# Sharing a convolution tap of every second chunk between ACT and GpSimd in a state-space scan (one core, fp32)

## The chip, the core and the metric

The kernel runs on one core of a Trainium2 chip. Its time is the device time of one execution in microseconds. The names of the engines are those of the profile: PE is TensorE, DVE is VectorE, ACT is ScalarE, POOL is GpSimd, and SP issues most of the DMAs. Each engine works through its own queue in order; they meet through semaphores.

## The reference

Eight sequences of 256 tokens of width 256 go through two layers. The part that matters here is the mixer of the first layer. Each token is projected to x (256 channels), B and C (32 heads of 64 states each) and a few more. The channels of x, B and C go through a causal convolution of four taps along the sequence:

```
def causal_conv1d(x, w, b):   # y[t] = w3 x[t] + w2 x[t-1] + w1 x[t-2] + w0 x[t-3] + b
```

Then comes the scan: with the running sums cum of the decays, each head takes scores[i, j] = exp(cum[i] - cum[j]) * (C[i] . B[j]) for j <= i, zero otherwise, and y = scores x. Gates, an output projection, a feed-forward block, LoRA experts, attention and a mixture of experts follow; the change does not touch them.

## The kernel before, in words

The 2048 tokens are worked in four rounds (`for r in range(ROUNDS)`) of 512 tokens, two sequences of 256. Channels lie on the partitions, tokens along the free axis, so that one chunk of 128 channels is a tile of 128x512. A head pair p (16 of them) needs two chunks of the convolution: ("BC", p, 0), the B channels of two heads, and ("BC", p, 1), the C channels. They are kept in `bc`, three pairs deep (`p % 3`), in SBUF.

The scan of a round has 32 steps, `steps[g]`, a head pair p and a sequence b each: (0,0), (0,1), (1,0), (1,1) and so on up to pair 13, then (14,0), (15,0), (14,1), (15,1). What each engine does in step g is written out by hand, one loop for each engine (the taps of the first two pairs come before the scan):

- SP (`broadcast_rows`, L793 to L804) loads the rows of running sums of step g into one of four buffers `crow[g % 4]`, and for that waits until the decays of step g-4 are done.
- POOL (L1529 to L1537) waits for that load and puts 1e30 above the diagonal with two `affine_select`, one per head. This is the mask; it counts up `masked`. POOL does nothing else in the scan.
- ACT (L1411 to L1416) takes `decay(g + 1)`, four exponentials over `crow` that wait for the masks of step g+1, and then `first_tap` for the chunk that PE projects in step g: out of PSUM, times the last tap's weight, plus the bias, into `bc`.
- PE (L1055 to L1076) takes the products C.B of step g (L1032, L1033), the projection of one chunk (`project_bc(p + 2, b)`: four matmuls of 128x512, L883), and in every second step `add_y` (L1048, L1051), which multiplies the scores with x. A projection goes to PSUM bank b, and for that the chunk before in that bank must be drained. The products of a pair wait until both of its chunks are drained.
- DVE (L1858 to L1880) multiplies the decays with the products (L1871, the score multiplication), then takes taps 2 and 3 of the chunk of step g-1, and then tap 1 of the chunk of step g. A tap (L1651) is one `scalar_tensor_tensor` that reads the projection from PSUM, shifted by s tokens, and adds it to `bc`; tap 1 waits for ACT's first tap, tap 3 drains the bank. At g = 20 and g = 31 half of the output and a quarter of it are written in front of the score multiplication (`output`, L1848, L1855).

Of the kernel before, what the change touches and what calls it, by code (L numbers as in the profile page):

```python
# [107 lines left out]
def sandwich(nc, A, out):  # L108
    with ExitStack() as ctx:
# [9 lines left out]
        def settle(eng):  # L119


            eng.sem_inc(settled, 1)
# [96 lines left out]

        sg = xc  # L220

        lg0 = sb("lg0", [P, TILES, EXPERTS0])
        mx = sb("mx", [P, TILES, 8])
        ix = sb("ix", [P, TILES, 8], U32)
# [172 lines left out]
        cum_ready = signal("cum_ready", 1)  # L397
        cum_out = sem("cum_out")
        crow_in = [sem(f"crow_in{i}") for i in range(CROWS)]
        decayed = signal("decayed", 64)  # L400
        masked = signal("masked", 64)
        y_added = signal("y_added", 64)
# [519 lines left out]
        def _(pe):  # L922
# [67 lines left out]
            for r in range(ROUNDS):  # L990
# [64 lines left out]
                for g in range(2 * PAIRS):  # L1055
                    p, b = steps[g]
                    ns = (2 * g, 2 * g + 1)
                    if b == 0:
                        for w in range(2):
                            pe.wait_ge(*plan.drained(("BC", p, w), r))  # L1060
                    pe.wait_ge(*plan.before(("CB", p, b), r))
                    for second in [products(n) for n in ns]:
                        mm = second()
                    mm.then_inc(plan.fills(("CB", p, b)), 1)
                    if p + 2 < PAIRS:
                        if p + 2 == PROJ_PAIRS[1] and b == 0:
                            pe.wait_ge(w_proj[2], 16)
                        project_bc(p + 2, b)
                    if g == 1:

                        for c in range(DC):
                            pe.wait_ge(*plan.before(("Y", c), r))
                            pe.matmul(plan[("Y", c)][:, :], zeros_bf[:, 0:P], zeros_bf[:, :], start=True,
                                      stop=False, skip_group_check=True).then_inc(plan.fills(("Y", c)), 1)
                    if g >= 1 and steps[g - 1][0] % 2 == 1:
                        add_y(*steps[g - 1])  # L1076
# [237 lines left out]
        def _(act):  # L1314
# [48 lines left out]
            for r in range(ROUNDS):  # L1363
                def first_tap(key, dst, j):
                    act.wait_ge(*plan.full(key, r))
                    act.activation(dst, plan[key][:, :], ACT.Identity, bias=conv_b[:, j:j + 1],  # L1366
                                   scale=conv_w[:, j, TAPS - 1:TAPS]).then_inc(tap0.sem, 1)

                for c in range(DC):
                    first_tap(("X", c), xc[:, c, :], c)  # L1370
                for w in range(2):
# [39 lines left out]
                for g in range(2 * PAIRS):  # L1411
                    p, b = steps[g]
                    if g + 1 < 2 * PAIRS:
                        decay(g + 1)
                    if p + 2 < PAIRS:
                        first_tap(("BC", p + 2, b), bc[:, (p + 2) % 3, b, :], 2 + 16 * b + p + 2)  # L1416

                if r > 1:
                    act.wait_ge(sh_out, 16 * (r - 1) + CREDIT)
# [69 lines left out]
        @block.gpsimd  # L1489
        def _(pool):  # L1490
            def power(n, cols, r):
                pool.wait_ge(var_ready.sem, var_ready.at(r, n))
                pool.tensor_tensor(rs[:, cols], ve[:, cols], half[:, cols], ALU.pow).then_inc(rstd_ready.sem, 1)  # L1493

            def ahead_power(r, n):
                pool.wait_ge(ahead_var.sem, ahead_var.at(r, n))
                pool.tensor_tensor(rs1[:, :], ve1[:, :], half[:, :], ALU.pow).then_inc(ahead_rstd.sem, 1)

            pool.memset(half[:, :], -0.5).then_inc(pads_zero, 1)
            pool.wait_ge(pads_zero, 1)  # L1500
            ahead_power(0, 1)
            ahead_power(0, 2)
            pool.memset(x_pad[:, :, :], 0.0).then_inc(pads_zero, 1)
            pool.memset(v_pad[:, :, :, :, :], 0.0).then_inc(pads_zero, 1)
            pool.memset(before[:, :, :], 0.0).then_inc(pads_zero, 1)
            pool.memset(xf[:, :, :], 0.0).then_inc(pads_zero, 1)
            pool.memset(table[:, :, :], 0.0).then_inc(pads_zero, 1)
            pool.memset(nmax[:, :, :, :], 0.0).then_inc(pads_zero, 1)
            for e in range(2):
                pool.memset(head_ones[:, e, 16 * e:16 * e + 16], 1.0).then_inc(pads_zero, 1)  # L1510
            pool.memset(head_ones[:, :, :].rearrange("p e d -> p (e d)")[:, 16:48], 0.0).then_inc(pads_zero, 1)
            pool.wait_ge(pads_zero, PADS)

            def spread_rows(d):
                pool.wait_ge(groups_ready.sem, groups_ready.at(d, 1))
                settle(pool)
                for h in range(2):
                    pool.tensor_tensor(oh_rows[:, :, h, :], in_group[:, :, :], row_parts[:, h, :].unsqueeze(2)
                                       .broadcast_to([P, TILES * TOPK, EGROUPS]), ALU.mult)\
                                           .then_inc(rows_ready.sem, 1)  # L1520
                pool.wait_ge(rows_ready.sem, rows_ready.at(d, 2))
                settle(pool)
                pool.tensor_scalar(row_parts[:, 0, :], row_parts[:, 0, :], float(GROUP * TOPK // 64), None, ALU.add)\
                    .then_inc(row_chain.sem, 1)
                pool.wait_ge(row_chain.sem, row_chain.at(d, 1))
                settle(pool)

            for r in range(ROUNDS):
                for g in range(2 * PAIRS):  # L1529

                    pool.wait_ge(crow_in[g % CROWS], (r * (2 * PAIRS // CROWS) + g // CROWS) * 16 + 16)
                    settle(pool)
                    for e in range(2):
                        diagonal = crow[g % CROWS][:, e, :].rearrange("p (b l) -> p b l", l=P)[:, 0:3:2, :]
                        pool.affine_select(diagonal, diagonal, pattern=[[0, 2], [1, P]], base=0,
                                           channel_multiplier=-1, compare_op=ALU.is_ge,
                                           fill=1e30).then_inc(masked.sem, 1)  # L1537
                def keep_causal(ks):


                    for k in ks:
                        pool.wait_ge(*plan.drained(("ST", k), r))
                        settle(pool)
                        for i in range(2):
                            x = prT[k % 6][:, i, 0:SEQ].rearrange("p (b n) -> p b n", n=P)
                            pool.affine_select(x, x, pattern=[[0, 2], [1, P]], base=0, channel_multiplier=-1,
                                               compare_op=ALU.is_ge, fill=0.0).then_inc(causal.sem, 1)

                att = len(POWERS) - 4
                for n in range(att):  # L1550
                    power(n + 1, POWERS[n], r)
                    if n == 1 and r > 0:
                        spread_rows(r - 1)
                keep_causal((0, 1))
                if r < LAST:
                    ahead_power(r + 1, 1)
                keep_causal((2,))
                if r < LAST:
                    ahead_power(r + 1, 2)
                keep_causal(range(3, 14))  # L1560
                power(att + 1, POWERS[att], r)
                keep_causal((14, 15))
                for n in range(att + 1, att + 4):
                    power(n + 1, POWERS[n], r)
            spread_rows(LAST)
            tail_pool(pool)
# [3 lines left out]
        def _(dve):  # L1570
# [69 lines left out]
            def tap(r, s, chunks, taps_done):  # L1640
# [7 lines left out]
                for n, (key, dst, j) in enumerate(chunks):  # L1648
                    d = dst.rearrange("p (b l) -> p b l", b=SEQS)[:, :, s:SEQ]
                    x = plan[key][:, :].rearrange("p (b l) -> p b l", b=SEQS)[:, :, 0:SEQ - s]  # L1650
                    ins = dve.scalar_tensor_tensor(d, x, conv_w[:, j, TAPS - 1 - s:TAPS - s], d,  # L1651
                                                   ALU.mult, ALU.add)
                    if s < TAPS - 1:
                        ins.then_inc(chain, 1)
                        count[0] += 1
                        last_tap[0] = count[0]
                    else:
                        ins.then_inc(plan.drains(key), 1)

            last_tap = [0]  # L1660

# [115 lines left out]
            for r in range(ROUNDS):  # L1777
# [80 lines left out]
                for g in range(2 * PAIRS):  # L1858
# [15 lines left out]
                    if g == 0:  # L1874
                        tap(r, TAPS - 1, [bc_chunk(1, w) for w in range(2)], taps_done)
                    if g >= 1 and (g - 1) // SEQS + 2 < PAIRS:
                        tap(r, 2, [bc_chunk((g - 1) // SEQS + 2, (g - 1) % SEQS)], taps_done)
                        tap(r, 3, [bc_chunk((g - 1) // SEQS + 2, (g - 1) % SEQS)], taps_done)
                    if p + 2 < PAIRS:
                        tap(r, 1, [bc_chunk(p + 2, b)], taps_done)  # L1880
                output(1, slice(SEQ, GROUP), 64)

# [330 lines left out]
```

## Time and profile before

| | us |
|---|---|
| median of 3 runs | 1291.43 (1290.85 to 1294.38) |
| the profiled execution, its own time | 1297.54 |
| its span, first to last instruction | 1295.5 |
| PE busy | 1110.3 (86% of the span) |
| DVE busy | 867.8 (67%) |
| ACT busy | 499.0 (39%) |
| POOL busy | 251.8 (19%) |
| mean granted clock of TensorE | 0.939 of full speed |

The shares are averages over stages that have different limits, so they say little about one stage. The span is 2.0 us shorter than the execution's own time, because it counts from the first instruction to the last. A granted clock of 1.00 is 2.4 GHz and one of 0.50 is 1.2 GHz.

### The profile page before, as it was taken

Reading aid. Unit: us, or ns where it says so; the run is one execution under the profiler, and the core shown is the slowest. Engines: PE = TensorE matmul, PEld = TensorE weight load, DVE = VectorE, ACT = ScalarE, POOL = GpSimd, SP = SyncE. Lnnn points to the kernel's source line nnn. Section 1 sums busy time; section 2 is a strip of 40 time slices with the busy share of each in tenths; the row PEclk is TensorE's granted clock in tenths of the full one; section 3 lists DMA queues with packets and bytes.
Section 4 is the critical chain, followed back from the end, with each engine's and each line's share of the span. In section 5 each row is a group of like instructions: output and inputs, shape, how many; then the busy total and the mean of one; then the engine's idle time right before and its main releaser. Section 6 shows DMA issues by size and latency. Waiting matters only on the chain.

```text
span 1295.5 us, 19826 instructions
## 1 busy us (share of the span) xinstructions
PE 1110.3 (86%) x7192; PEld 672.5 (52%) x7192; DVE 867.8 (67%) x1848; ACT 499.0 (39%) x1076; POOL 251.8 (19%) x522
## 2 busy tenths in 40 slices
PE   3999896888998997888998997888998997886667
PEld 1444554554445675554445674554445675465345
DVE  5899526669997545669996636769997546565126
ACT  2766411236665202246665102236664111221133
POOL 3222001132221000222221000222221000222432
PEclk9999998899999997899999997899999997897679
DMA  5888100004431000004331000004348030035345
GB/s 177 284 266 282 36 1 16 1 2 133 120 116 59 1 8 26 2 2 146 121 120 41 1 17 17 1 5 155 122 123 216 4 94 21 2 81 167 118 162 186
DMA packets 72673, 111.75 MB, mean 86 GB/s; under 512 B 5896, under 2 KB 62608, under 8 KB 71682
## 3 DMA queue, kind: packets, MB, share of 16 engines
q1 hardware_dynamic: 68738, 98.51, 24.4%
q10 hardware_dynamic: 2304, 8.39, 2.0%
q0 software_dynamic: 1536, 3.60, 0.9%
q8 instruction: 57, 0.93, 0.3%
q14 instruction: 38, 0.31, 0.1%
HBM read 91.81 MB, written 19.27 MB: 86 GB/s over the span
## 4 chain that ended last, share of the span: by engine, by line
PE 61%; DVE 20%; issue 7%; ACT 6%; DMA 2%; another core or an unknown queue 1%; POOL 1%; DVEq 0%; SPq 0%; POOLq 0%; ACTq 0%
PE bank L883 22%; DVE hf L1651 5%; PE bank L948 4%; PE bank L1124 4%; PE bank L1165 3%; PE bank L1032 3%; PE bank L1048 2%; DVE nmax L2041 2%; PE bank L962 2%; PE bank L1211 2%; DVE u L1871 2%; PE bank L1208 2%; PE bank L896 2%; DMA out_dram<-tmp 2%
## 5 line engine op out<-in xcount | busy, mean ns | idle before, releaser
L883 PE MATMUL bank<-uT,w_in 128*128 128x512 f32 (+1 forms) x584 | 288.2, 621 | 25.0 <-DVE hf L1651 11.3
L1651 DVE SCALAR_TENSOR_TENSOR hf<-bank,conv_w,hf 128x510 f32<-128x510 f32 (+2 forms) x384 | 277.9, 743 | 18.5 <-ACT hf L1366 13.3
L883 PEld LDWEIGHTS bank<-uT,w_in 128*128 128x128 f32 (+1 forms) x584 | 99.9, 188 | 123.3 <-issue 90.1
L1366 ACT ACTIVATE hf<-bank,conv_b,conv_w 128x512 f32<-128x512 f32 x128 | 99.4, 777 | 136.6 <-PE bank L883 136.6
L1493 POOL TENSOR_TENSOR rs<-ve,half 128x2 f32<-128x2 f32 x56 | 39.0, 697 | 382.1 <-DVE ve L1783 382.1
L1032 PE MATMUL bank<-hf 64*128 64x256 f32 x512 | 89.7, 426 | 12.6 <-issue 7.2
L883 PE MATMUL bank<-uT,w_gu 128*128 128x512 f32 x224 | 99.0, 593 | 0.0
L2041 DVE TENSOR_REDUCE nmax<-bank 128x2 f32<-128x256 f32 (+1 forms) x128 | 65.4, 554 | 44.1 <-PE bank L1211 44.1
L1032 PEld LDWEIGHTS bank<-hf 64*128 64x128 f32 x512 | 38.8, 184 | 69.8 <-issue 63.5
L1871 DVE TENSOR_TENSOR turned_p<-dec,bank 128x768 f32<-128x768 f32 x64 | 60.9, 952 | 15.9 <-PE bank L1033 5.0
L1346 ACT ACTIVATE xc<-bank 128x512 f32<-128x512 f32 x44 | 26.3, 597 | 115.3 <-PE bank L883 77.1
L883 PEld LDWEIGHTS bank<-uT,w_gu 128*128 128x128 f32 x224 | 42.3, 190 | 46.6 <-issue 45.9
L1901 DVE TENSOR_TENSOR hf<-xc,bank 128x512 f32<-128x512 f32 x32 | 22.0, 687 | 62.8 <-PE bank L883 44.6
L1124 PE MATMUL bank<-w_dn,hf 128*128 128x256 f32 x256 | 56.2, 380 | 3.6 <-issue 3.6
L948 PE MATMUL bank<-uT_moe,w_sgu 128*128 128x256 f32 x256 | 58.7, 384 | 0.0
L874 PE MATMUL bank<-ident,u 128*128 128x128 f32 x128 | 23.9, 318 | 39.6 <-DVE u L1607 17.1
L948 PEld LDWEIGHTS bank<-uT_moe,w_sgu 128*128 128x128 f32 x256 | 49.6, 194 | 12.1 <-issue 5.7
L1124 PEld LDWEIGHTS bank<-w_dn,hf 128*128 128x128 f32 x256 | 48.3, 190 | 13.2 <-issue 6.8
L1033 PEld LDWEIGHTS bank<-hf 64*128 64x128 f32 x512 | 50.0, 187 | 5.3
L1463 ACT ACTIVATE dec<-bank 128x768 f32<-128x768 f32 x32 | 26.0, 811 | 64.2 <-PE bank L1222 64.2
L1463 ACT ACTIVATE turned_p<-bank 128x768 f32<-128x768 f32 x24 | 19.5, 811 | 80.6 <-PE bank L1222 80.6
L1033 PE MATMUL bank<-hf 64*128 64x128 f32 x512 | 49.9, 270 | 0.0
(314 smaller groups left out, 2174.9 us busy)
## 6 DMA issues: line engine op xcount, KB each, us to landing
hf<-cum_dram SPq DMA_DIRECT2D x32, 384.0 KB, 3.7
dec<-cum_dram SPq DMA_DIRECT2D x32, 384.0 KB, 3.6
tmp<-cum_dram SPq DMA_DIRECT2D x32, 384.0 KB, 3.6
x<-cum_dram SPq DMA_DIRECT2D x32, 384.0 KB, 3.5
y_dram<-xf SPq DMA_DIRECT2D x16, 512.0 KB
hf<-y_dram ACTq DMA_DIRECT2D x16, 512.0 KB, 4.5
w_in<-in_w_in SPq DMA_DIRECT2D x1, 3584.0 KB, 12.0
w_in<-in_w_egu SPq DMA_DIRECT2D x6, 512.0 KB, 9.2
```

Of the source, the lines that this page charges most:

```text
L883: mm = pe.matmul(plan[key][0:n, :], w[:, k, cols], uT[:, k, :], start=k == 0, stop=k == DC - 1)
L948: mm = pe.matmul(plan.of(key, d)[:, i * HALF:(i + 1) * HALF], w_sgu[:, k, o + i * P:o + (i + 1) * P], uT_moe[:, k, j * HALF:(j + 1) * HALF ...
L1032: pe.matmul(cb[:, e, 0:SEQ], B[:, o:o + P], C[:, o:o + SEQ], start=True, stop=True)
L1033: return lambda: pe.matmul(cb[:, e, SEQ:TRI], B[:, o + P:o + SEQ], C[:, o + P:o + SEQ], start=True, stop=True)
L1124: mm = pe.matmul(plan[("F", j)][:, i * D:(i + 1) * D], hf[:, f, t * P:(t + 1) * P], w_dn[:, f, :], start=f == 0, stop=f == FF // P - 1)
L1165: mm = pe.matmul(plan[key][:, cols], w_att[:, k, n, c * P:(c + 1) * P], uT[:, k, cols], start=k == 0, stop=k == DC - 1)
L1366: act.activation(dst, plan[key][:, :], ACT.Identity, bias=conv_b[:, j:j + 1], scale=conv_w[:, j, TAPS - 1:TAPS]).then_inc(tap0.sem, 1)
L1463: act.activation(prT[k % 6], pair_banks(("ST", k))[:, :, 0:TRI], ACT.Exp)\
L1493: pool.tensor_tensor(rs[:, cols], ve[:, cols], half[:, cols], ALU.pow).then_inc(rstd_ready.sem, 1)
L1651: ins = dve.scalar_tensor_tensor(d, x, conv_w[:, j, TAPS - 1 - s:TAPS - s], d, ALU.mult, ALU.add)
L1871: dve.tensor_tensor(sc[g % 4], dec[:, d:d + 2, :], both_cb[g % 2][:, :, 0:TRI], ALU.mult).then_inc(plan.drains(("CB", p, b)), 1)
L2041: ins = dve.tensor_reduce(nmax[:, n // 4 % 2, i, col:col + 33:32], S[:, :, cols], AX.X, ALU.max, negate=True)
```

## The change

For each C chunk of pairs 2 to 15 (b = 1, 14 a round) the tap furthest back, tap 3, leaves DVE. ACT multiplies the projection with the tap's weight right behind `first_tap` of the same chunk, into a buffer `last_product` (a part of `yg`, one buffer for all chunks, so from the second chunk of a round on ACT waits for the addition of the chunk before). POOL adds this product to the chunk in SBUF; it does so in the even steps g from 2 to 28, behind the mask of step g and in front of the mask of step g+1, for the chunk that PE projects in step g-1, and it waits for ACT's product and for DVE's last tap of that chunk. DVE takes taps 1 and 2 of such a chunk both in step g, and tap 2 drains the bank. The B chunks keep their order. PE waits for the addition before the products of a pair (`conv_sum`).

```diff
--- before.py
+++ after.py
@@ -218,6 +218,8 @@
         cum_tok = sb("cum_tok", [P, TILES, HEADS])
 
         sg = xc
+
+        last_product = yg[:, 1, :].rearrange("p (b l) -> p b l", b=SEQS)[:, :, TAPS - 1:SEQ]
 
         lg0 = sb("lg0", [P, TILES, EXPERTS0])
         mx = sb("mx", [P, TILES, 8])
@@ -397,6 +399,8 @@
         cum_ready = signal("cum_ready", 1)
         cum_out = sem("cum_out")
         crow_in = [sem(f"crow_in{i}") for i in range(CROWS)]
+        tap3 = signal("tap3", PAIRS - 2)
+        conv_sum = signal("conv_sum", PAIRS - 2)
         decayed = signal("decayed", 64)
         masked = signal("masked", 64)
         y_added = signal("y_added", 64)
@@ -1058,6 +1062,8 @@
                     if b == 0:
                         for w in range(2):
                             pe.wait_ge(*plan.drained(("BC", p, w), r))
+                        if p >= 2:
+                            pe.wait_ge(conv_sum.sem, conv_sum.at(r, p - 1))
                     pe.wait_ge(*plan.before(("CB", p, b), r))
                     for second in [products(n) for n in ns]:
                         mm = second()
@@ -1366,6 +1372,14 @@
                     act.activation(dst, plan[key][:, :], ACT.Identity, bias=conv_b[:, j:j + 1],
                                    scale=conv_w[:, j, TAPS - 1:TAPS]).then_inc(tap0.sem, 1)
 
+                def tap_product(p):
+
+                    key = ("BC", p, 1)
+                    if p > 2:
+                        act.wait_ge(conv_sum.sem, conv_sum.at(r, p - 2))
+                    x = plan[key][:, :].rearrange("p (b l) -> p b l", b=SEQS)[:, :, 0:SEQ - TAPS + 1]
+                    act.activation(last_product, x, ACT.Copy, scale=conv_w[:, 18 + p, 0:1]).then_inc(tap3.sem, 1)
+
                 for c in range(DC):
                     first_tap(("X", c), xc[:, c, :], c)
                 for w in range(2):
@@ -1414,6 +1428,8 @@
                         decay(g + 1)
                     if p + 2 < PAIRS:
                         first_tap(("BC", p + 2, b), bc[:, (p + 2) % 3, b, :], 2 + 16 * b + p + 2)
+                        if b == 1:
+                            tap_product(p + 2)
 
                 if r > 1:
                     act.wait_ge(sh_out, 16 * (r - 1) + CREDIT)
@@ -1535,6 +1551,14 @@
                         pool.affine_select(diagonal, diagonal, pattern=[[0, 2], [1, P]], base=0,
                                            channel_multiplier=-1, compare_op=ALU.is_ge,
                                            fill=1e30).then_inc(masked.sem, 1)
+                    p = (g - 2) // SEQS + 2
+                    if g >= 2 and g % 2 == 0 and p < PAIRS:
+
+                        pool.wait_ge(tap3.sem, tap3.at(r, p - 1))
+                        pool.wait_ge(*plan.drained(("BC", p, 1), r))
+                        settle(pool)
+                        x = bc[:, p % 3, 1, :].rearrange("p (b l) -> p b l", b=SEQS)[:, :, TAPS - 1:SEQ]
+                        pool.tensor_tensor(x, x, last_product, ALU.add).then_inc(conv_sum.sem, 1)
                 def keep_causal(ks):
 
 
@@ -1657,6 +1681,14 @@
                     else:
                         ins.then_inc(plan.drains(key), 1)
 
+            def tap_and_drain(r, s, key, dst, j):
+
+                dve.wait_ge(chain, last_tap[0])
+                d = dst.rearrange("p (b l) -> p b l", b=SEQS)[:, :, s:SEQ]
+                x = plan[key][:, :].rearrange("p (b l) -> p b l", b=SEQS)[:, :, 0:SEQ - s]
+                dve.scalar_tensor_tensor(d, x, conv_w[:, j, TAPS - 1 - s:TAPS - s], d, ALU.mult, ALU.add)\
+                    .then_inc(plan.drains(key), 1)
+
             last_tap = [0]
 
             def sum_dt(r):
@@ -1874,9 +1906,15 @@
                     if g == 0:
                         tap(r, TAPS - 1, [bc_chunk(1, w) for w in range(2)], taps_done)
                     if g >= 1 and (g - 1) // SEQS + 2 < PAIRS:
-                        tap(r, 2, [bc_chunk((g - 1) // SEQS + 2, (g - 1) % SEQS)], taps_done)
-                        tap(r, 3, [bc_chunk((g - 1) // SEQS + 2, (g - 1) % SEQS)], taps_done)
-                    if p + 2 < PAIRS:
+                        p2, b2 = (g - 1) // SEQS + 2, (g - 1) % SEQS
+                        if b2 == 0:
+                            tap(r, 2, [bc_chunk(p2, b2)], taps_done)
+                            tap(r, 3, [bc_chunk(p2, b2)], taps_done)
+                        else:
+                            dve.wait_ge(tap3.sem, tap3.at(r, p2 - 1))
+                            tap(r, 1, [bc_chunk(p2, b2)], taps_done)
+                            tap_and_drain(r, 2, *bc_chunk(p2, b2))
+                    if p + 2 < PAIRS and b == 0:
                         tap(r, 1, [bc_chunk(p + 2, b)], taps_done)
                 output(1, slice(SEQ, GROUP), 64)
 
```

## Rows read from the trace of the kernel before

**Rows 1.** The page's head.
```profile
span 1295.5 us, 19826 instructions
```

**Rows 2.** Stretch table: us, busy PE, PEld, DVE, ACT, POOL, granted clock, DMA
```profile
315.20:412.00 96.80, 91.21 (x600) 46.30 (x600) 90.06 (x121) 64.53 (x152) 21.51 (x56) 1.00 0.37 115
```

**Rows 3.** The chain that ended last, round 1: start us, us, engine, tile, line
```profile
388.87 1.98 PE bank L883 x4
390.85 0.57 PE bank L1048 x8
391.42 0.22 PE bank L1051 x8
391.64 0.63 PE bank L1032 x4
392.27 0.22 PE bank L1033 x4
392.50 1.91 PE bank L883 x4
```

**Rows 4.** DVE timeline, round 1: start us, us, line, operation, count
```profile
321.00 0.94 DVE L1871 TENSOR_TENSOR u<-dec,bank 128x768 f32<-128x768 f32 x1
...
379.11 0.74 DVE L1848 SCALAR_TENSOR_TENSOR yg<-xc,chan,bank 128x512 f32<-128x512 f32 x1
...
380.50 0.95 DVE L1871 TENSOR_TENSOR turned_p<-dec,bank 128x768 f32<-128x768 f32 x1
...
387.30 2.18 DVE L1651 SCALAR_TENSOR_TENSOR hf<-bank,conv_w,hf 128x508 f32<-128x508 f32 x3
389.39 0.94 DVE L1871 TENSOR_TENSOR h<-dec,bank 128x768 f32<-128x768 f32 x1
...
392.60 0.95 DVE L1871 TENSOR_TENSOR turned_p<-dec,bank 128x768 f32<-128x768 f32 x1
393.47 1.52 DVE L1651 SCALAR_TENSOR_TENSOR hf<-bank,conv_w,hf 128x508 f32<-128x508 f32 x2
395.26 0.75 DVE L1651 SCALAR_TENSOR_TENSOR hf<-bank,conv_w,hf 128x510 f32<-128x510 f32 x1 [0.27 <-ACT hf L1366]
...
405.64 0.95 DVE L1871 TENSOR_TENSOR turned_p<-dec,bank 128x768 f32<-128x768 f32 x1
...
410.03 0.95 DVE L1871 TENSOR_TENSOR u<-dec,bank 128x768 f32<-128x768 f32 x1
```

**Rows 5.** ACT's timeline in the same stretch
```profile
394.45 0.78 ACT L1366 ACTIVATE hf<-bank,conv_b,conv_w 128x512 f32<-128x512 f32 x1 [1.39 <-PE bank L883]
395.13 0.50 ACT L1405 ACTIVATE dec<-tmp,cum_tok 128x256 f32<-128x256 f32 x1
...
395.82 0.49 ACT L1405 ACTIVATE dec<-tmp,cum_tok 128x256 f32<-128x256 f32 x1
```

**Rows 6.** POOL's timeline in the same stretch
```profile
386.98 0.77 POOL L1535 TENSOR_SCALAR_AFFINE_SELECT tmp<-tmp 128x256 f32<-128x256 f32 x2 [2.74 <-DMA tmp<-cum_dram]
```

**Rows 7.** Groups by form, POOL, then ACT: count, busy us, mean ns, idle
```profile
L1518 POOL TENSOR_TENSOR oh_rows<-in_group,row_parts 128x256 bf16<-128x256 f32 x8 | 4.8, 623 | 74.4 <-DVE in_group L1728 74.4
...
L1523 POOL TENSOR_SCALAR row_parts<-row_parts 128x16 f32<-128x16 f32 x4 | 1.0, 262 | 0.8 <-POOL oh_rows L1518 0.8
...
L1366 ACT ACTIVATE hf<-bank,conv_b,conv_w 128x512 f32<-128x512 f32 x128 | 99.4, 777 | 136.6 <-PE bank L883 136.6
...
L1322 ACT ACTIVATE uT<-bank 128x512 f32<-128x512 f32 x16 | 9.5, 595 | 72.2 <-PE bank L874 72.2
```

**Rows 8.** Timeline of a handoff from DVE to POOL, after the scan
```profile
474.57 0.17 DVE L1783 TENSOR_SCALAR ve<-mv 128x2 f32<-128x2 f32 x1
474.82 0.72 POOL L1493 TENSOR_TENSOR rs<-ve,half 128x2 f32<-128x2 f32 x1 [32.15 <-DVE ve L1783]
```

**Rows 9.** Stretch table, PE's pause behind the scan of round 1
```profile
418.40:420.40 2.00, 0.84 (x6) 0.47 (x5) 1.11 (x5) 0.68 (x4) 0.74 (x2) 1.00 0.00 0
...
420.80:424.40 3.60, 3.60 (x12) 3.03 (x13) 0.62 (x2) 2.12 (x3) 0.00 (x0) 0.55 0.00 0
```

## The prediction

> Notation: step g of the scan is what each engine does for steps[g]; c(g) is the chunk projected in step g (even g: a B chunk, b = 0; odd g: a C chunk, b = 1).
>
> **What bounds it now.** I read the page's head, then the stretch table, the chain, and last the timelines of one engine at a time. The profiled execution has a span of 1295.5 us [rows 1]. The scan of round 1 fills 96.8 us of it and the other three look the same: PE is busy for 91.21 us, DVE for 90.06, at 2.4 GHz throughout (granted clock 1.00) [rows 2]. So two engines are nearly full, and a tap less on DVE looks like a gain. The chain says how much: it alternates between DVE and long stretches of PE, so PE has almost nothing to give. A projection takes PE 1.91 to 1.98 us, the products 0.63 + 0.22, a Y addition 0.57 + 0.22 [rows 3]. A pair of steps holds two projections, two pairs of products and one addition: 2 x 1.92 + 2 x 0.85 + 0.79 = 6.33 us. The real pace is (405.64 - 321.00) / 13 = 6.51 us per pair, from the score multiplication (L1871) of step 2 to that of step 28 [rows 4]. With DVE for nothing the scan could win 0.18 us a pair.
>
> The distances from which I build [rows 4]: score multiplication to the first tap behind it 0.87 us (392.60 to 393.47); tap to tap 0.70 (three from 387.30 to 389.39); two taps to the end of the second 1.52. ACT [rows 5]: from a decay's first exponential to what follows the fourth 1.38 (two heads of 0.69 each, 395.13 to 395.82), a first tap 0.78, and 0.03 from its end (395.23) to the DVE tap that waits for it (395.26).
>
> What nobody waits for today is POOL. Its masks run far ahead: the mask of step 26 starts at 386.98 [rows 6], and ACT reads it at 395.13 [rows 5], while DVE is only between steps 22 and 23. That lead of 8.1 us is what the change spends.
>
> **The change, part by part.**
> DVE loses tap 3 of one chunk in each pair: 14 a round, 0.70 us each, 39 us in 56 pairs. At most 0.18 of each 0.70 could have counted.
>
> ACT gains 14 products a round, 128x506 from PSUM. Not in the trace; bounds are the plain copy of 128x512, 0.595, and the tap with scale and bias, 0.777 [rows 7]. I take 0.68. It stands behind first_tap(g) of odd steps, before a decay whose cover is good for more than that (below), so it costs nothing here; without that cover it would be up to 0.78 x 56 = 44 us.
>
> POOL gains 14 additions a round of 128x506 f32 with two inputs. The nearest two-input row is L1518, 128x256, 0.623 us; a 128x16 operation takes 0.262 [rows 7]. So 0.262 + 506 / 256 x (0.623 - 0.262) = 0.97 us. Below, it is not cheaper than a mask of half its size with one input, 0.41; above, not more than twice L1518, 1.25. L1518 does not have the addition's shape, so both ends stay in the range.
> The Trainium skill (GPSIMD Engine Reference, section 3.1) speaks against this move: elementwise work with two inputs is about twice as slow on GpSimd, 4497 ns for 2048 f32 columns; that would make the addition some 1.11 us by an estimate, and the sum 8 us longer.
>
> The price lies in where the addition stands. POOL's queue is in order: mask(g), then for even g from 2 to 28 the wait for DVE's last tap of c(g-1), the addition, and only then mask(g+1). DVE issues that last tap in step g, behind the score multiplication of g. So queued behind POOL's new wait is mask(g+1); behind it on ACT decay(g+1); behind that, in ACT's order, first_tap(g); and for that waits DVE's tap 1 of c(g), which in DVE's order stands before the score multiplication of g+1. This is a loop through three engines, without slack. From the start of the score multiplication of an even g:
> - tap 1 and tap 2 of c(g-1): 0.87 + 1.52 = 2.39
> - to POOL 0.08, as a small DVE result reaches POOL today (474.74 to 474.82) [rows 8], and the addition 0.97: 3.44
> - first half of mask(g+1) 0.41, to ACT 0.03: 3.88
> - decay(g+1) 1.38: 5.26
> - first_tap(g) 0.78, to DVE 0.03: 6.07
> - tap 1 of c(g) 0.70: 6.77, score multiplication of g+1 0.87: 7.64
> - tap 2 and tap 3 of c(g) 1.40: 9.04, and the next pair begins.
> So 9.04 us a pair instead of 6.51.
>
> Is anything else late in such a pair? decay(g+2) runs on ACT from 6.04 to 7.4, and first_tap(g+1) and the product from 7.4 to 8.9, before the 9.9 at which DVE asks for them. PE waits for conv_sum until 3.44, in front of the products of g+2, which nobody needs before 9.04. PE's projection of c(g+2) waits for the bank, which tap 3 of c(g) frees at about 9.1; then PE has 6.33 us of work in 9.04 and stands still for 2.7. SP's row loads for step g+4 go out after decay(g), as today, and are masked more than a pair later; they remain hidden, though all masks are late.
>
> Per round: 13 pairs x 9.04 = 117.5 in place of 84.64. Once a round DVE writes half of the output before step 20, 1.39 us (379.11 to 380.50) [rows 4]; it stands in the loop now and adds all of it: 118.9, so +34.3. From step 28 to 30: decay(29) ends at about 5.3, decay(30) behind it at 6.7, so the score multiplication of 30 stands at 6.74 instead of 410.03 - 405.64 = 4.39 [rows 4]: +2.35. Step 1 loses a tap before the loop begins: -0.70. Sum 35.9, in four rounds 144 us. Nothing outside the scan changes.
>
> The profiled execution took 1297.5 us, 6 above the median of the runs, and would take 1441; from the median, 1291.4 + 144 = **1435 us**.
>
> **Rivals.**
> - *The clock falls and PE becomes the bound.* After 2.00 us in which PE was busy for 0.84 at a granted clock of 1.00, a stretch of 3.6 us had 0.55 on average, near 1.2 GHz [rows 9]. The new gap of 2.7 us is of that kind. One such fall, 3.6 to 4 us long, costs PE some 2 us of work, less than its 2.7 us of slack, so I charge nothing. If it lasted for the whole of every pair, PE would need 12.66 us a pair: 52 x 3.62 = 188 more, 1623 us; in half of the pairs, about 1529. Against that: PE is dense for over 6 us once it starts, and the 0.55 is above 0.50, so the clock rose again before that stretch was over, in which PE was busy throughout [rows 9]. Chance 0.08. [...]
> - *The addition is much dearer than L1518 suggests*, 2 us say: 56 x 1.03 = 58 more, 1493 us. Chance 0.05.
> - *Faster: POOL stays ahead.* The taps, the product and the addition all lie beside PE's work, and PE bounds at 6.33: 52 x 0.18 = 9 us less, 1282. It decides if mask(g+1) is there when ACT asks for it. ACT begins a decay before DVE begins the step in front of it; by my table the mask comes 3.85 us after that begins. For it stand DVE's and PE's shares of the scan; against it, the order of POOL's queue. Chance 0.03; that the two effects cancel to no change (within 0.3%, about what a measurement of this kernel can tell) 0.02.
>
> **Numbers.** Forecast 0.82: 1435 us, and from 1404 (addition 0.41: 56 x 0.56 less) to 1451 (1.25: 56 x 0.28 more). Handoffs that I left out, 0.05 to 0.2 us a pair, add up to 11, and clock falls that reach the loop in part take it further. The range goes from 1404 to 1495; that leaves out the faster cases, the worst of the clock and a little of the rest. Slower by over 0.3%: 0.95, the same 0.02, faster 0.03.
>
> **What would show it.** Score multiplications in pairs of 9 us, the shorter part (about 2.3) after odd steps, the longer (6.8) after even ones. POOL's masks of odd steps directly behind the new addition, whose wait is put down to DVE's tap; a long wait of ACT's exponentials for POOL masks, and of DVE's tap 1 for ACT's first tap. POOL in the chain, in which it hardly appears now. PE's share of the scan falls from 94% to about 70%. Wrong if the masks of odd steps still run a step ahead of ACT; if the pair is PE from end to end; or if the addition takes well over 1.25 us.

## The result, and the profile after

| | before | changed | ratio |
|---|---|---|---|
| median of 4 runs, us | 1291.14 | 1454.66 | 1.127 (1.123 to 1.131) |

The change costs 163.5 us; 144 were predicted (1435 us), the range of 1404 to 1495 holds the result. I follow the profile in the order in which the prediction was built. The page's head first: its span and the busy time of each engine.

```profile
span 1452.9 us, 20030 instructions
...
PE 1161.8 (80%) x7172; PEld 692.9 (48%) x7192; DVE 829.2 (57%) x1792; ACT 525.3 (36%) x1132; POOL 315.6 (22%) x578
```

DVE has become 39 us less busy, as meant (867.8 before), and the span 157 us longer. An engine that is freed without being what the others wait for gives nothing back. PE's busy time grew by 51 us although its work is the same: that is the lower clock, below. In the chain that ended last PE's share fell from 61% to 42%, and those of DVE (20% to 27%), ACT (6% to 14%) and POOL (1% to 3%) grew.

The stretch table, with the same columns as [rows 2]. First the 13 pairs of round 1; then the pair of that round in which the clock was lowest and which took longest (the pair with half of the output aside), one in which it did not fall, one in which it fell for a shorter part, and the last pair, in which it did not fall either.

```profile
364.07:487.53 123.46, 96.23 (x536) 44.80 (x536) 70.16 (x94) 62.31 (x143) 35.05 (x65) 0.89 0.25 82
392.16:401.72 9.56, 9.38 (x41) 4.24 (x41) 5.37 (x9) 4.46 (x11) 2.69 (x5) 0.67 0.28 89
401.72:411.09 9.37, 6.33 (x40) 3.09 (x40) 5.29 (x7) 5.21 (x12) 2.70 (x5) 1.00 0.23 77
411.09:420.46 9.37, 8.01 (x40) 3.47 (x40) 5.28 (x8) 4.78 (x11) 2.70 (x5) 0.82 0.25 80
...
478.17:487.53 9.36, 7.25 (x56) 3.56 (x56) 5.27 (x8) 4.77 (x11) 2.70 (x5) 1.00 0.23 80
```

From step 2 to step 28 a round takes 123.46 us instead of 84.64 [rows 4]. An undisturbed pair takes 9.37 us (9.04 predicted), and in it PE is busy for 6.33, the work that the prediction had added up for it (most pairs at full clock read 6.39). No engine is full: the pair is a chain of waits. Here it is, DVE's timeline of that pair:

```profile
401.72 0.95 DVE L1903 TENSOR_TENSOR u<-dec,bank 128x768 f32<-128x768 f32 x1
402.59 0.74 DVE L1675 SCALAR_TENSOR_TENSOR hf<-bank,conv_w,hf 128x510 f32<-128x510 f32 x1
403.37 0.75 DVE L1689 SCALAR_TENSOR_TENSOR hf<-bank,conv_w,hf 128x508 f32<-128x508 f32 x1
408.13 0.75 DVE L1675 SCALAR_TENSOR_TENSOR hf<-bank,conv_w,hf 128x510 f32<-128x510 f32 x1 [4.01 <-ACT hf L1372]
408.79 0.94 DVE L1903 TENSOR_TENSOR h<-dec,bank 128x768 f32<-128x768 f32 x1
409.65 1.52 DVE L1675 SCALAR_TENSOR_TENSOR hf<-bank,conv_w,hf 128x508 f32<-128x508 f32 x2
411.09 0.94 DVE L1903 TENSOR_TENSOR turned_p<-dec,bank 128x768 f32<-128x768 f32 x1
```

then POOL's timeline, and ACT's:

```profile
404.29 1.26 POOL L1561 TENSOR_TENSOR hf<-hf,yg 128x506 f32<-128x506 f32 x1 [6.88 <-DVE hf L1689]
405.50 0.77 POOL L1551 TENSOR_SCALAR_AFFINE_SELECT x<-x 128x256 f32<-128x256 f32 x2
```

```profile
405.94 0.51 ACT L1419 ACTIVATE dec<-x,cum_tok 128x256 f32<-128x256 f32 x1 [3.79 <-POOL x L1551]
...
407.33 0.76 ACT L1372 ACTIVATE hf<-bank,conv_b,conv_w 128x512 f32<-128x512 f32 x1
```

L1903 is the score multiplication, L1675 a tap, L1689 the last tap of a C chunk, L1561 the addition, L1551 the mask, L1419 the first of the exponentials, L1372 the first tap. Read across: DVE ends tap 2 at 404.12; POOL, which had nothing to do for 6.88 us, adds; the mask of the next step follows; ACT has waited 3.79 us for it; behind the decay comes the first tap, for which DVE has waited 4.01 us. The next score multiplication stands 7.07 us after the one before, and the one behind it 2.30 us later: the long and the short part of the pair that the prediction gave as 6.8 and 2.3.

The groups by line show the two new operations, and the waits show that this happens in nearly every pair (56 additions):

```profile
L1561 POOL TENSOR_TENSOR hf<-hf,yg 128x506 f32<-128x506 f32 x56 | 70.3, 1256 | 412.9 <-DVE hf L1689 412.9
...
L1381 ACT ACTIVATE yg<-bank,conv_w 128x506 f32<-128x506 f32 x56 | 37.5, 670 | 0.0
```

```profile
DVE hf L1675 <- ACT hf L1372: 211.6, 56, 4.0
...
ACT dec L1419 <- POOL dec L1551: 134.6, 28, 6.0
ACT dec L1419 <- POOL x L1551: 124.2, 28, 4.7
```

### The profile page after: what moved, and what is told of

It is laid out like the page before. It is cut to its first block, busy times and chain, and to the rows that moved or that the text cites. A ratio compares the mean times of both kernels' runs of the same rounds, so it can differ in the third digit from the quotient of the medians.

```text
span 1452.9 us, 20030 instructions
## 1 busy us (share of the span) xinstructions
PE 1161.8 (80%) x7172; PEld 692.9 (48%) x7192; DVE 829.2 (57%) x1792; ACT 525.3 (36%) x1132; POOL 315.6 (22%) x578
## 4 chain that ended last, share of the span: by engine, by line
PE 42%; DVE 27%; ACT 14%; issue 11%; POOL 3%; DMA 2%; POOLq 1%; DVEq 0%; SPq 0%; ACTq 0%
PE bank L887 11%; DVE hf L1675 6%; ACT dec L1419 4%; PE bank L952 4%; ACT dec L1421 4%; DVE turned_p L1903 3%; PE bank L1130 3%; DVE hf L1689 3%; PE bank L1171 3%; ACT hf L1372 3%; DVE nmax L2079 2%; DVE h L1903 2%; PE bank L1217 2%; PE bank L966 2%; PE bank L1214 1%
## 5 line engine op out<-in xcount | busy, mean ns | idle before, releaser
L887 PE MATMUL bank<-uT,w_in 128*128 128x512 f32 (+1 forms) x584 | 321.8, 683 | 118.0 <-DVE hf L1675 105.9
L1675 DVE SCALAR_TENSOR_TENSOR hf<-bank,conv_w,hf 128x510 f32<-128x510 f32 (+2 forms) x272 | 199.8, 743 | 214.8 <-ACT hf L1372 211.6
L887 PEld LDWEIGHTS bank<-uT,w_in 128*128 128x128 f32 (+1 forms) x584 | 107.6, 202 | 226.5 <-DVE hf L1675 116.5
L1561 POOL TENSOR_TENSOR hf<-hf,yg 128x506 f32<-128x506 f32 x56 | 70.3, 1256 | 412.9 <-DVE hf L1689 412.9
L1036 PE MATMUL bank<-hf 64*128 64x256 f32 x512 | 99.8, 469 | 23.9 <-POOL hf L1561 18.6
L1372 ACT ACTIVATE hf<-bank,conv_b,conv_w 128x512 f32<-128x512 f32 x128 | 97.8, 764 | 24.2 <-PE bank L887 24.1
L1036 PEld LDWEIGHTS bank<-hf 64*128 64x128 f32 x512 | 43.6, 207 | 88.3 <-issue 82.0
L1419 ACT ACTIVATE dec<-dec,cum_tok 128x256 f32<-128x256 f32 x64 | 32.0, 499 | 134.6 <-POOL dec L1551 134.6
L1419 ACT ACTIVATE dec<-x,cum_tok 128x256 f32<-128x256 f32 x64 | 32.0, 499 | 124.2 <-POOL x L1551 124.2
L1903 DVE TENSOR_TENSOR turned_p<-dec,bank 128x768 f32<-128x768 f32 x64 | 60.5, 946 | 19.0 <-PE bank L1037 14.3
L1037 PEld LDWEIGHTS bank<-hf 64*128 64x128 f32 x512 | 54.7, 205 | 7.6
```

Of the source, the lines that this page charges most:

```text
L887: mm = pe.matmul(plan[key][0:n, :], w[:, k, cols], uT[:, k, :], start=k == 0, stop=k == DC - 1)
L1036: pe.matmul(cb[:, e, 0:SEQ], B[:, o:o + P], C[:, o:o + SEQ], start=True, stop=True)
L1037: return lambda: pe.matmul(cb[:, e, SEQ:TRI], B[:, o + P:o + SEQ], C[:, o + P:o + SEQ], start=True, stop=True)
L1419: act.activation(dec[:, n % 4, 0:SEQ], crow[g % CROWS][:, e, 0:SEQ], ACT.Exp, bias=cum_tok[:, 2 * b, h:h + 1], scale=-1.0)
L1561: pool.tensor_tensor(x, x, last_product, ALU.add).then_inc(conv_sum.sem, 1)
L1903: dve.tensor_tensor(sc[g % 4], dec[:, d:d + 2, :], both_cb[g % 2][:, :, 0:TRI], ALU.mult).then_inc(plan.drains(("CB", p, b)), 1)
```

## Experiments

The theory to be tested: the time is the loop DVE's last tap, POOL's addition, mask, ACT's decay, ACT's first tap, DVE's tap 1, and it exists only because of the order in POOL's queue. The rival: it is the added work itself, on ACT and POOL, or what it does to the others in SBUF. Two of the kernels leave a part of the computation out; their expectations say which. The ratios are to the kernel before as it ran beside each experiment: 1289.0 us for the first four kernels below, 1290.2 us for the last three.

**POOL takes the addition three masks later** (changed kernel):

```diff
-                    p = (g - 2) // SEQS + 2
-                    if g >= 2 and g % 2 == 0 and p < PAIRS:
+                    h = g - 3
+                    p = (h - 2) // SEQS + 2
+                    if h >= 2 and h % 2 == 0 and p < PAIRS:
```

> POOL takes each addition three steps later in its own order, behind the mask of step g+3 instead of that of step g; all the work of the change stays. Loop theory (mask of g+1 stuck behind the addition): the loop is gone, PE bounds the pair at 6.33 us, about 1282 us. Load theory (the time is the added work on ACT and POOL, or their traffic in SBUF): the work is the same, so it stays above 1400 us.

Measured: 1289.5 us, ratio to the kernel before 1.000 (0.998 to 1.002). All of the 163 us are gone with the work unchanged. The load theory is out. The expected 1282 us did not come; the time is 7 us above it. Its DVE timeline, the score multiplications of steps 14, 16 and 18 of round 1, and POOL's timeline:

```profile
360.41 0.95 DVE L1904 TENSOR_TENSOR u<-dec,bank 128x768 f32<-128x768 f32 x1 [0.38 <-PE bank L1037]
...
366.73 0.95 DVE L1904 TENSOR_TENSOR turned_p<-dec,bank 128x768 f32<-128x768 f32 x1 [0.61 <-PE bank L1037]
...
373.06 0.95 DVE L1904 TENSOR_TENSOR u<-dec,bank 128x768 f32<-128x768 f32 x1 [0.38 <-PE bank L1037]
```

```profile
344.01 1.27 POOL L1562 TENSOR_TENSOR hf<-hf,yg 128x506 f32<-128x506 f32 x1 [2.67 <-DVE hf L1690]
345.24 0.76 POOL L1551 TENSOR_SCALAR_AFFINE_SELECT hf<-hf 128x256 f32<-128x256 f32 x2
```

Two pairs in 12.65 us: 6.32 each, and what DVE waits for are PE's products (L1037). So PE bounds the pair, at the value predicted for that case. The 13 pairs of a round take 82.5 us instead of 84.64. What was won there is lost at the end of the round: the four last score multiplications spread over 10.12 us in round 1 (9.08 to 10.12 in the four rounds) instead of 6.38. DVE's and PE's timelines of that place, and two stretches:

```profile
404.67 0.95 DVE L1904 TENSOR_TENSOR turned_p<-dec,bank 128x768 f32<-128x768 f32 x1 [0.61 <-PE bank L1037]
...
414.79 0.95 DVE L1904 TENSOR_TENSOR h<-dec,bank 128x768 f32<-128x768 f32 x1 [0.59 <-PE bank L1037]
```

```profile
408.74 1.22 PE L1036 MATMUL bank<-hf 64*128 64x256 f32 x4 [3.39 <-POOL hf L1562]
```

```profile
404.00:406.00 2.00, 1.35 (x24) 0.77 (x20) 1.39 (x3) 1.97 (x6) 0.72 (x2) 1.00 0.00 0
...
410.00:412.00 2.00, 2.00 (x16) 1.46 (x18) 1.19 (x2) 0.46 (x2) 0.00 (x0) 0.50 0.00 0
```

Step 29 is the first of head pair 15, whose C chunk is the last one added. There is no projection left to fill the time, so PE stands still for 3.39 us until that addition is there, and the granted clock falls to 0.50, that is 1.2 GHz. In the kernel before, PE stood still for 1.81 us in front of the same products, and the clock stayed at 1.00:

```profile
408.14 0.70 PE L1032 MATMUL bank<-hf 64*128 64x256 f32 x4 [1.81 <-issue]
```

**One mask later only** (the same edit with `h = g - 1`):

> The addition one step later only, between the mask of g+1 and that of g+2. Loop theory: the mask of g+2 would come 4.2 us after the score multiplication of g, ACT asks for it at about 5.3, so nothing is late: about 1282 us, the same as with three masks ahead. Rival (any coupling of POOL to DVE's taps is harmful): between 1300 and 1400 us. Load theory: above 1400 us.

Measured: 1291.5 us, ratio 1.002 (1.000 to 1.003); 1282 were expected, and again the end of the round is what is missing. One mask ahead is as good as three within 0.2%, and nothing of the loop is left (the 13 pairs take 82.9 us): tying POOL to DVE's taps does no harm as long as the next mask is out first. This kernel also happens to separate the two parts of the end of a round. PE's wait for the last addition was as long in round 1 as in round 2 (PE's timeline), but of these two only in round 1 did the clock fall in the stretch from step 28 to step 31 (stretch table); it fell in rounds 0 and 1 and not in 2 and 3:

```profile
409.35 1.23 PE L1036 MATMUL bank<-hf 64*128 64x256 f32 x4 [3.39 <-POOL hf L1562]
...
696.19 0.70 PE L1036 MATMUL bank<-hf 64*128 64x256 f32 x4 [3.40 <-POOL hf L1562]
```

```profile
405.27:415.19 9.92, 6.53 (x57) 4.56 (x50) 5.17 (x7) 5.00 (x14) 2.69 (x5) 0.66 0.01 2
692.11:700.07 7.96, 4.12 (x57) 3.00 (x50) 5.00 (x7) 5.00 (x14) 2.69 (x5) 1.00 0.01 2
```

Against 6.38 us before, the wait is worth 1.6 us, and the clock another 2.0 where it falls.

**The addition cut to 8 of 506 columns** (changed kernel):

```diff
-                        x = bc[:, p % 3, 1, :].rearrange("p (b l) -> p b l", b=SEQS)[:, :, TAPS - 1:SEQ]
-                        pool.tensor_tensor(x, x, last_product, ALU.add)
+                        x = bc[:, p % 3, 1, :].rearrange("p (b l) -> p b l", b=SEQS)[:, :, TAPS - 1:TAPS + 3]
+                        pool.tensor_tensor(x, x, last_product[:, :, 0:4], ALU.add)
```

> As the changed kernel, but POOL adds only the first 4 columns of each sequence (8 of 506), so most of tap 3 of the C chunks is left out; every wait stays. Loop theory: the addition falls from 1.26 to about 0.26 us and each of 56 loops gets shorter by it: 56 us less, about 1398 us. If the addition were covered: no change, 1455 us.

Measured: 1400.1 us, ratio 1.087 (1.083 to 1.090), 54.6 less than the changed kernel. The group of the addition and two score multiplications of even steps on DVE's timeline:

```profile
L1561 POOL TENSOR_TENSOR hf<-hf,yg 128x8 f32<-128x8 f32 x56 | 11.6, 206 | 411.3 <-DVE hf L1689 411.3
```

```profile
365.37 0.94 DVE L1903 TENSOR_TENSOR u<-dec,bank 128x768 f32<-128x768 f32 x1
...
373.70 0.95 DVE L1903 TENSOR_TENSOR turned_p<-dec,bank 128x768 f32<-128x768 f32 x1
```

The addition is 1.05 us shorter and the pair 1.04 (8.33): it lies in the loop with its whole length. The part that was cut is a third of what the change costs (54.6 of 163.5 us); the rest is there with hardly any addition.

**The wait alone** (kernel before, all taps on DVE):

```diff
                                            fill=1e30).then_inc(masked.sem, 1)
+                    p = (g - 2) // SEQS + 2
+                    if g >= 2 and g % 2 == 0 and p < PAIRS:
+                        pool.wait_ge(*plan.drained(("BC", p, 1), r))
```

> The kernel before, its taps all on DVE, with one thing added: in even steps POOL waits for DVE's last tap of the C chunk before it takes the next mask. No product, no addition. Loop theory: pair of 8.8 us (2.39 to the end of tap 3, 0.17 to POOL, 0.44 to ACT, 2.19 to DVE's tap 1, 0.66 to the next score multiplication, 2.96 to the one after it), 52 x 2.3 + some 10 = about 1421 us. Load theory: 1291 us, nothing was added that takes time.

Measured: 1426.6 us, ratio 1.106 (1.103 to 1.109). A wait that computes nothing costs 138 us (the kernel before took 1289.0 beside it). POOL's timeline and DVE's:

```profile
368.03 0.77 POOL L1535 TENSOR_SCALAR_AFFINE_SELECT dec<-dec 128x256 f32<-128x256 f32 x2 [7.40 <-DVE hf L1654]
```

```profile
365.39 0.94 DVE L1874 TENSOR_TENSOR turned_p<-dec,bank 128x768 f32<-128x768 f32 x1
366.26 1.52 DVE L1654 SCALAR_TENSOR_TENSOR hf<-bank,conv_w,hf 128x508 f32<-128x508 f32 x2
...
371.32 0.94 DVE L1874 TENSOR_TENSOR turned_p<-dec,bank 128x768 f32<-128x768 f32 x1
374.28 0.94 DVE L1874 TENSOR_TENSOR u<-dec,bank 128x768 f32<-128x768 f32 x1
```

A pair of 8.89 us (5.93 + 2.96), 8.8 expected; the difference is the handoff from DVE's last tap, which ends at 367.78, to POOL at 368.03, 0.25 us and not 0.17. This is the sharpest test: the same loop without any of the change's work.

**ACT takes the first tap before the decay** (changed kernel, from step 2 on):

```diff
+                    if p + 2 < PAIRS and b == 0 and g >= 2:
+                        first_tap(("BC", p + 2, b), bc[:, (p + 2) % 3, b, :], 2 + 16 * b + p + 2)
                     if g + 1 < 2 * PAIRS:
                         decay(g + 1)
-                    if p + 2 < PAIRS:
+                    if p + 2 < PAIRS and (b == 1 or g < 2):
                         first_tap(("BC", p + 2, b), bc[:, (p + 2) % 3, b, :], 2 + 16 * b + p + 2)
```

> The changed kernel, but from step 2 on ACT takes the first tap of a B chunk in front of the decay of g+1 instead of behind it. POOL's order and all work stay. Loop theory: first tap and DVE's tap 1 (0.8 + 0.66 us) leave the loop, the decay's end (about 5.7 us after the score multiplication of g) leads straight to the score multiplication of g+1: pair 5.73 + 2.30 = 8.03 instead of 9.37, 52 x 1.34 = 70 less, about 1385 us. Rival (only POOL's queue counts, ACT's order does not): 1455 us.

Measured: 1385.6 us, ratio 1.075 (1.071 to 1.078), 69 less than the changed kernel (70 expected). ACT's timeline, the first tap now in front of the decay, and DVE's, with the pair of 8.04:

```profile
364.95 0.78 ACT L1372 ACTIVATE hf<-bank,conv_b,conv_w 128x512 f32<-128x512 f32 x1 [1.88 <-PE bank L887]
...
367.00 0.51 ACT L1419 ACTIVATE dec<-x,cum_tok 128x256 f32<-128x256 f32 x1 [1.27 <-POOL x L1553]
```

```profile
362.79 0.94 DVE L1905 TENSOR_TENSOR u<-dec,bank 128x768 f32<-128x768 f32 x1
...
370.83 0.95 DVE L1905 TENSOR_TENSOR turned_p<-dec,bank 128x768 f32<-128x768 f32 x1
```

So the first tap and tap 1 were members of the loop through ACT's order alone; ACT is busy for 5.21 of the 9.37 us of an undisturbed pair of the changed kernel.

**The last pair left as it was** (kernel with three masks ahead; the edit in its conditions, `tap3` and `conv_sum` count one less a round):

```diff
-                        if p >= 2:
+                        if 2 <= p < PAIRS - 1:
                             pe.wait_ge(conv_sum.sem, conv_sum.at(r, p - 1))
...
-                        if b == 1:
+                        if b == 1 and p + 2 < PAIRS - 1:
                             tap_product(p + 2)
...
-                    if h >= 2 and h % 2 == 0 and p < PAIRS:
+                    if h >= 2 and h % 2 == 0 and p < PAIRS - 1:
...
-                        if b2 == 0:
+                        if b2 == 0 or p2 == PAIRS - 1:
...
-                    if p + 2 < PAIRS and b == 0:
+                    if p + 2 < PAIRS and (b == 0 or p + 2 == PAIRS - 1):
```

> The kernel with three masks ahead, and the C chunk of the last pair (15) keeps its tap 3 on DVE, so no product, no addition and no wait of PE for it. Theory of the end of the round: with three masks ahead the scan gains 2.15 + 0.65 us a round, and loses them because PE stands still for the last addition and goes on at half the clock; without that addition the end takes the 6.38 us of before: 4 x 2.8 = 11 us less than before, about 1278 us. Rival (the gain is lost elsewhere, behind the scan): 1289 us, as before.

Measured: 1282.9 us, ratio 0.994 (0.993 to 0.996). It beats both kernels, by 7.3 us against the one before; the difference is only 0.6%, but its interval leaves out 1. On DVE's timeline, the end of round 1, steps 28 to 31:

```profile
400.40 0.95 DVE L1904 TENSOR_TENSOR turned_p<-dec,bank 128x768 f32<-128x768 f32 x1
...
403.91 0.95 DVE L1904 TENSOR_TENSOR turned_p<-dec,bank 128x768 f32<-128x768 f32 x1 [1.12 <-PE bank L1037]
404.78 0.95 DVE L1904 TENSOR_TENSOR u<-dec,bank 128x768 f32<-128x768 f32 x1
...
406.78 0.95 DVE L1904 TENSOR_TENSOR h<-dec,bank 128x768 f32<-128x768 f32 x1
```

6.38 us again, as before the change, and the 13 pairs take 82.5 us. The trace has the expected 2.8 us less in each scan (11 in all); of them 7.3 show in the median, and the expected 1278 us was missed by 5. Where the other 4 stay I did not find. In the profiled executions the time outside the four scans differs by as much where the program is the same: 898.9 us with three masks ahead, 903.7 here, 908.2 in the kernel before.

**Tap 3 of the C chunks left out** (kernel before):

```diff
+                        p2, b2 = (g - 1) // SEQS + 2, (g - 1) % SEQS
+                        if b2 == 0:
+                            tap(r, 2, [bc_chunk(p2, b2)], taps_done)
+                            tap(r, 3, [bc_chunk(p2, b2)], taps_done)
+                        else:
+                            tap_and_drain(r, 2, *bc_chunk(p2, b2))
```

> The kernel before without tap 3 of the C chunks of pairs 2 to 15 (left out of the computation); nothing takes its place, DVE drains the bank with tap 2. It is the most that the change could win. Theory (PE bounds the pair at 6.33 us): at most 2.15 us in the pairs of a round and little at its ends, 1278 to 1282 us. If DVE bounded the scan: 56 x 0.70 = 39 us less, 1250 us.

Measured: 1276.7 us, ratio 0.989 (0.987 to 0.991). With the taps gone for nothing, a third of their 39 us comes through, 14. That is 1.3 us below the expected 1278 to 1282: the 13 pairs win 2.8 us a round (81.85 in place of 84.65), 2.15 were allowed, and the end of the round 0.8 (5.60 in place of 6.38), "little" was allowed. Two pairs on DVE's timeline take 12.64 us, PE's floor again:

```profile
357.18 0.95 DVE L1879 TENSOR_TENSOR u<-dec,bank 128x768 f32<-128x768 f32 x1
...
369.82 0.94 DVE L1879 TENSOR_TENSOR u<-dec,bank 128x768 f32<-128x768 f32 x1
```

## Why the prediction was right, and where its size was off

- **The loop** was the right mechanism, with the members and the order that were given. The wait alone, the three masks ahead and ACT's swapped order each change one link and move the time as it says.
- **Its terms**, predicted and measured, from the score multiplication of an even step: end of tap 2 at 2.39 and 2.40; POOL begins at 2.47 and 2.57; the next mask begins at 3.44 and 3.78; ACT at 3.88 and 4.22; the first tap at 5.26 and 5.61; DVE's tap 1 at 6.07 and 6.41; the next score multiplication at 6.77 and 7.07; the pair ends at 9.04 and 9.37.
- **The term that was mis-sized is the addition**: 0.97 us estimated from L1518 [rows 7], 1.256 measured, just outside the upper end of 1.25. By the two shapes that ran here, 8 and 506 columns, it takes 0.206 us plus 2.1 ns per further column; the prediction's scaling of L1518 took 1.4 ns. (It divided by 256 columns where its two rows lie 240 apart; with 240 it is 1.5 ns and 1.00 us, still short: the nearest row misled.) The handoff to POOL was 0.17 us, not 0.08. Both together are 0.33 us a pair, 52 x 0.33 = 17 us. The Trainium skill (GPSIMD Engine Reference, section 3.1) gives 4497 ns for an addition of 2048 f32 columns, by an estimate 2.2 ns per column. The trace agrees in the price of a column, 2.1 ns; the 1.11 us that the prediction worked out from that figure was nearer than 0.97 and 0.15 short.
- **The end of the round** was predicted with 2.35 us more than before and measured with 3.4 to 3.9. Of the difference 0.33 us a round are the two terms above once more. For the rest, the step that failed is "PE waits for conv_sum until 3.44, in front of the products of g+2, which nobody needs before 9.04": right inside the scan, wrong at step 29, where the next products already belong to the last chunk. PE stood still there for 4.5 to 4.8 us, the clock fell, and DVE then waited for PE's slow products. All in all some 5 us in four rounds. The last addition is not the only thing that holds PE there: with the wait alone, where PE waits for no addition, it stood still for 3.58 us at that place in every round, the clock fell, and the end took 8.80 us in two rounds and 7.70 in two. The shares of the two in the changed kernel were not taken apart. PE's timeline in round 1, the changed kernel, then the wait alone:

```profile
491.60 1.22 PE L1036 MATMUL bank<-hf 64*128 64x256 f32 x4 [4.51 <-POOL hf L1561]
```

```profile
476.19 1.22 PE L1032 MATMUL bank<-hf 64*128 64x256 f32 x4 [3.58 <-issue]
```

- **The clock** was charged with nothing. It did fall inside the scan, to an average of 0.89 in round 1. In most of the pairs in which it fell it stood at 0.82 to 0.84 on average, PE's work swelled from 6.33 to about 8 us, and the pair took 9.36 or 9.37 us all the same. In two pairs of round 1 it stood at 0.67, and these took 9.50 and 9.56 us, with PE busy for 9.26 and 9.38. PE's slack of 3 us took the rest, so the rival in which PE becomes the bound did not happen, though in the longest pair PE was as good as full. About 0.2 us a round. For the same reason PE's share of the scan of round 1 fell to 78% and not to about 70%.
- These make 144 + 17 + 5 + 1 = 167, against 163.5 between the medians. In the traces the four scans, from the score multiplication of step 0 to that of step 31, take 554.2 us in place of 387.3, 166.9 more: the sum holds where the change works. The two profiled spans differ by 157; what follows the last scan was 9 us shorter in the profile after, which the change does not touch (the profiled execution before was itself 6 us above its median).
- **The product on ACT**: 0.67 us (0.68 taken), and free, as said; the kernels with one and with three masks ahead carry all 56 and take 1291.5 and 1289.5 us.
- **The faster rival** (POOL stays ahead, 1282 us) was priced right as a mechanism: when POOL does stay ahead, a pair takes 6.32 us (6.33). It just is not this change, which needs another order in POOL's queue, and at the end of the round the last chunk left alone.

## What to carry to other kernels

Before moving work to an idle engine, look at what stands behind it in that engine's queue: the idle engine here was a prefetcher, and its lead of 8 us was the thing of value. A wait put in front of a prefetched step ties all who need that step to the one waited for, even where the moved work costs nothing. Put the moved work behind at least the next prefetched step (one did as much here as three) and in time for its own deadline, and look at the first and last turns of the loop by themselves, since there the cover is missing.

## What was not expected of the hardware

The same pause of PE, 3.39 and 3.40 us before the same instruction of one kernel, was followed by a fall of the granted clock in one round (0.66 over the stretch) and by none in the other (1.00). In the scan of round 1 of the changed kernel PE has seven pauses of 2.72 to 3.18 us in front of a projection. In or behind six of them the clock fell to 0.50 for a while, behind the last, of 2.97 us, it did not; behind the pauses of 1.2 to 1.5 us it did not fall either. PE's timeline, a pause with a fall behind it and the one without (their stretches, from 411.09 and from 478.17, stand in the table above):

```profile
411.23 2.95 PE L887 MATMUL bank<-uT,w_in 128*128 128x512 f32 x4 [3.18 <-DVE hf L1675]
...
478.30 1.98 PE L887 MATMUL bank<-uT,w_in 128*128 128x512 f32 x4 [2.97 <-DVE hf L1675]
```

So a fall has to be allowed for behind such a pause, but did not come behind every one. Its price was 2 us where nothing covered it (9.92 against 7.96), and from nothing to 0.2 us where PE had 3 us to spare.
